# Routing without the permutation matmul: each expert's logit folded to its own and its mapped place, and the soft matmuls of the first pass moved behind both sums

## The reference

```
scores = softmax(x @ gate_w.T)                    # 64 experts
topk_w, topk_idx = top_k(scores, 8)
w_e = zeros.at[topk_idx].add(topk_w)              # the 8 largest stay, at ties the lower index
flat = w_e[:, inv_map]                            # 8 groups x 8, an index map given as input
scalar = flat.sum(-1)                             # per group
soft = softmax(where(flat == 0, -1e9, flat))      # per group
xg = x + soft @ mask_up_w                         # per group
g, u = xg @ gate_proj_w.T, xg @ up_proj_w.T       # per group, 352 inner features
y = sum over groups of scalar * ((silu(g) * u) @ down_proj_w.T)
```

## Time and profile before

| | us |
|---|---|
| median of 3 runs | 1885.43 (1883.06 to 1886.68) |
| profiled execution | 1883.3 |
| its span | 1881.6 |
| TensorE busy | 1856.3 (99%) |
| VectorE busy | 802.2 (43%) |
| ScalarE busy | 528.2 (28%) |
| GpSimd busy | 140.0 (7%) |
| mean granted TensorE clock | 0.997 |

### The profile page before, as it was taken

How to read it: one execution, slowest core, us unless ns; L and a number is a source line. 1 busy time by engine, 2 the same in 40 slices (tenths; PEclk the granted TensorE clock), 3 DMA queues, 4 the chain that set the end, 5 groups by cost and what they waited for, 6 DMA issues and landing times.

```text
span 1881.6 us, 22831 instructions
## 1 busy us (share of the span) xinstructions
PE 1856.3 (99%) x8896; PEld 1552.5 (83%) x8896; DVE 802.2 (43%) x1478; ACT 528.2 (28%) x802; POOL 140.0 (7%) x246
## 2 busy tenths in 40 slices
PE   6999999999999999999999999999999999999999
PEld 5887888888888888888888888888888888888887
DVE  6455553545354543323334455354544323322222
ACT  3333423433124432112212533123432111311111
POOL 1131110100000000000010000000000000000000
PEclk9999999999999999999999999999999999999999
DMA  6987875445564455576676454564455566567665
GB/s 198 318 279 247 276 283 199 154 156 179 191 232 151 159 172 193 193 248 210 210 254 222 164 193 163 188 231 168 156 173 179 200 239 214 210 214 261 220 235 175
DMA packets 94187, 390.68 MB, mean 208 GB/s; under 512 B 11936, under 2 KB 12320, under 8 KB 71552
## 3 DMA queue, kind: packets, MB, share of 16 engines
q1 hardware_dynamic: 54096, 286.74, 43.1%
q10 hardware_dynamic: 27600, 47.15, 9.6%
q0 software_dynamic: 12384, 55.32, 7.8%
HBM read 347.36 MB, written 41.81 MB: 207 GB/s over the span
## 4 chain that ended last, share of the span: by engine, by line
PE 94%; DVE 3%; DMA 1%; ACT 1%; issue 1%; SPq 0%; ACTq 0%; DVEq 0%
PE bank L1012 27%; PE bank L1014 27%; PE bank L1013 27%; PE bank L1244 4%; PE bank L1022 1%; PE bank L1185 1%; PE bank L1177 1%; PE bank L1184 1%; DMA b_all<-wgu 1%; PE bank L1171 1%; DVE act_t L655 0%; PE bank L1042 0%; PE bank L1229 0%; PE bank L1043 0%; PE bank L1230 0%
## 5 line engine op out<-in xcount | busy, mean ns | idle before, releaser
L1012 PE MATMUL bank<-x_hi,wt 128*128 128x512 f32 x1328 | 525.2, 395 | 0.2 <-issue 0.2
L1014 PE MATMUL bank<-x_lo,wt 128*128 128x512 f32 x1328 | 518.5, 390 | 0.0
L1013 PE MATMUL bank<-x_hi,wt 128*128 128x512 f32 x1328 | 518.2, 390 | 0.0
L655 DVE TENSOR_TENSOR act_t<-bank,sig 128x512 f32<-128x512 f32 x176 | 121.6, 691 | 557.9 <-PE bank L1244 556.3
L1014 PEld LDWEIGHTS bank<-x_lo,wt 128*128 128x128 f32 x1328 | 249.5, 188 | 53.0
L1012 PEld LDWEIGHTS bank<-x_hi,wt 128*128 128x128 f32 x1328 | 249.8, 188 | 49.9 <-issue 0.6
L1013 PEld LDWEIGHTS bank<-x_hi,wt 128*128 128x128 f32 x1328 | 249.9, 188 | 49.1
L1012 PE MATMUL bank<-dt,a_hi 128*128 128x512 f32 x704 | 279.7, 397 | 0.3 <-DVE a_lo L655 0.3
L1014 PE MATMUL bank<-dt,a_hi 128*128 128x512 f32 x704 | 275.4, 391 | 0.0
L1013 PE MATMUL bank<-dt,a_lo 128*128 128x512 f32 x704 | 274.6, 390 | 0.0
L581 ACT ACTIVATE sig<-bank 128x512 f32<-128x512 f32 x176 | 105.3, 598 | 479.4 <-PE bank L1244 479.4
(11 more groups left out here) (178 smaller groups left out, 1748.5 us busy)
## 6 DMA issues: line engine op xcount, KB each, us to landing
wt<-scr_w SPq DMA_DIRECT2D x154, 1152.0 KB, 5.2
dt<-scr_d SPq DMA_DIRECT2D x154, 512.0 KB, 5.2
s_bc<-scr_s ACTq DMA_DIRECT2D x128, 256.0 KB, 5.3
state<-wat POOLq DMA_DIRECT2D x28, 512.0 KB, 5.3
scr_w<-wt POOLq DMA_DIRECT2D x12, 1024.0 KB, 5.1
b_all<-wgu SPq DMA_DIRECT2D x22, 512.0 KB, 7.4
scr_d<-dt POOLq DMA_DIRECT2D x22, 512.0 KB, 7.1
scr_w<-tw POOLq DMA_DIRECT2D x10, 1024.0 KB, 4.7
```

Source lines behind the costliest of these rows:

```text
L655: return nc.vector.tensor_tensor(dst, a, b, op)
L1012: mm(dst, wh, xh, start=start, stop=False)
L1013: mm(dst, wl, xh, start=False, stop=False)
L1014: return mm(dst, wh, xl, start=False, stop=stop)
```

## The change

`fold_m` gets 128 columns: in the first 64, as before, the sum of both halves of the logits; in the other 64 the logit of the expert that `inv_map` puts at that place. So VectorE has own and mapped logits side by side, and the turn, its copy, the permutation matmul and the copy out of PSUM (k = 43, 44) go. The top 8 are found on the own probabilities. A mapped probability stays if it is above the eighth largest, or equal to it with an index low enough (`rank`, `cut`). The probabilities are twice as wide, and `rank` and the wider `perm_i` are loaded and prepared at the start.

In pass 0 the soft matmul of the gate moves behind the up sum. SyncE loads the gate/up tile of the next chunk ahead of the down tile of this one. The m part of chunk 2 is made in round 0 and not in round 1. The loads of x for blocks 1 and 2 move from chunks 2 and 4 to 4 and 7. The first attention slab is loaded ahead of the stores of finished blocks (`first_slab`).

```diff
-        fold_m = sb("fold_m", [P, E])
+        fold_m = sb("fold_m", [P, 2 * E])
...
+            raw_gate_up(0)
+            raw_down(0)
             sp.dma_start(mask.rearrange("p a b -> p (a b)"), c_mask).then_inc(ld_mask, 16)
-            raw(1)
+            raw_gate_up(1)
+            raw_down(1)
+            raw_gate_up(2)
             for c in range(2, CH):
-                raw(c)
-                if c == 2:
-                    sp.dma_start(xr(1), x_t[1]).then_inc(ld_x[1], 16)
-                if c == 4:
-                    sp.dma_start(xr(2), x_t[2]).then_inc(ld_x[2], 16)
+                if c + 1 < CH:
+                    raw_gate_up(c + 1)
+                raw_down(c)
+                if c in (4, 7):
+                    b = (4, 7).index(c) + 1
+                    sp.dma_start(xr(b), x_t[b]).then_inc(ld_x[b], 16)
...
             for q in range(1, PHASES):
+                if q in ATT:
+                    first_slab(ATT[q])
                 if FINAL[q - 1]:
                     store_out(q - 1)
...
+            act.dma_start(rank[:, 0, :], c_rank.partition_broadcast(P)).then_inc(ld_perm, 16)
...
                     round_a(n)
+                    if n == 0:
+                        m_top(2)
...
-                    tt(r_b, logits, bcast(mx, E), ALU.subtract).then_inc(rmax_ok, 1)
+                    tt(probs, logits, bcast(mx, 2 * E), ALU.subtract).then_inc(rmax_ok, 1)
                 elif k == 41:
+                    own, mapped = probs[:, :, 0:E], probs[:, :, E:2 * E]
+                    stt = nc.vector.scalar_tensor_tensor
                     dve.wait_ge(exp_ok, p + 1)
-                    step(nc.vector.tensor_reduce(sm, r_b, AX.X, ALU.add))
+                    step(nc.vector.tensor_reduce(sm, own, AX.X, ALU.add))
                     step(nc.vector.reciprocal(sm, sm))
-                    step(tt(r_a, r_b, bcast(sm, E), ALU.mult))
+                    step(tt(probs, probs, bcast(sm, 2 * E), ALU.mult))
...
-                    tt(r_c, r_a, r_b, ALU.subtract).then_inc(top_ok, 1)
+                    for i in range(NT):
+                        ins = stt(r_a[:, i, :], r_b[:, i, :], top[:, i, TOPK - 1:TOPK], rank[:, 0, :], ALU.is_equal, ALU.mult)
+                    step(ins)
+                    for i in range(NT):
+                        stt(r_c[:, i, :], mapped[:, i, :], top[:, i, TOPK - 1:TOPK], mapped[:, i, :], ALU.is_gt, ALU.mult)
+                    step(nc.vector.tensor_reduce(cut[:], r_a, AX.X, ALU.max))
+                    for i in range(NT):
+                        ins = stt(r_a[:, i, :], rank[:, 1, :], cut[:, i:i + 1], mapped[:, i, :], ALU.is_gt, ALU.mult)
+                    step(ins)
+                    for i in range(NT):
+                        ins = stt(r_a[:, i, :], r_a[:, i, :], top[:, i, TOPK - 1:TOPK], r_a[:, i, :], ALU.is_ge, ALU.mult)
+                    step(ins)
+                    step(tt(r_c, r_c, r_a, ALU.max))
                 elif k == 44:
-                    dve.wait_ge(flat_ok, p + 1)
-                    step(nc.vector.tensor_copy(r_c, W1[:, 0:NT * E].rearrange("p (t e) -> p t e", t=NT)))
...
                     gate(n)
+                    if n == 0:
+                        m_mask(2)
                     pieces(3 * n + 1)
                     rest_a(n)
+                    if n == 0:
+                        m_rest(2)
...
                     for i in range(NT):
-                        ins = mm(W1[:, cols(i, E)], lgT[:, cols(i)], fold_m[:], start=True, stop=True)
+                        ins = mm(W1[:, cols(i)], lgT[:, cols(i)], fold_m[:], start=True, stop=True)
                     ins.then_inc(folded, 1)
-                elif k == 43:
-                    pe.wait_ge(top_ok, p + 1)
-                    for i in range(NT):
-                        ins = nc.tensor.transpose(W1[0:E, cols(i)], r_c[:, i, :], ident[:])
-                    ins.then_inc(wT_ok, 1)
-                elif k == 44:
-                    pe.wait_ge(wT_cp, p + 1)
-                    for i in range(NT):
-                        ins = mm(W1[:, cols(i, E)], w_eT[:, cols(i)], perm[:], start=True, stop=True)
-                    ins.then_inc(flat_ok, 1)
...
-                    soft(g_bank(n), 0, p, c).then_inc(g_ok, 1)
+                    if p:
+                        soft(g_bank(n), 0, p, c).then_inc(g_ok, 1)
                     pieces(3 * n)
                     if n > 1:
                         pe.wait_ge(t1_ok, n if n > 2 else 1)
                         main(UB, P, p, c)
+                    if p == 0:
+                        soft(g_bank(n), 0, p, c).then_inc(g_ok, 1)
                     soft(u_bank(n), P, p, c).then_inc(u_ok, 1)
```

More of the change, by code:

```diff
@@ L96, in build @@
         ident = sb("ident", [P, P])
-        fold_m = sb("fold_m", [P, E])
+        fold_m = sb("fold_m", [P, 2 * E])
         reset = sb("reset", [P, NB])
[L99 to L102, removed]
+        perm_i = sb("perm_i", [P, E], I32)
+        perm_w = sb("perm_w", [P, E])
+        rank = sb("rank", [P, 2, E])
+        iota = sb("iota", [P, 1])
+        cut = sb("cut", [P, NT])
         stats = sb("stats", [P, NT, 6])
@@ L141, in build @@
         tb_flat = tb[:].rearrange("p a b -> p (a b)")
[L142 to L145, removed]
+        probs = tb_flat[:, 0:2 * NT * E].rearrange("p (t e) -> p t e", t=NT)
+        r_a, r_b, r_c = (tb_flat[:, i * NT * E:(i + 1) * NT * E].rearrange("p (t e) -> p t e", t=NT) for i in range(2, 5))
+        route = tb_flat[:, 5 * NT * E:5 * NT * E + NT * 2 * P].rearrange("p (t c) -> p t c", t=NT)
+        lgT = tb_flat[:, 5 * NT * E + NT * 2 * P:5 * NT * E + NT * 2 * P + NB]
         e_pos, e_neg, e_rest = tb[:, 0:2, :], tb[:, 2:4, :], tb[:, 4:6, :]
@@ L245, in _, with raw_gate_up @@
         def _(sp):
-            def raw(c):
+            def raw_gate_up(c):
                 j, half = c // 2, c % 2
@@ L249, in raw, with raw_down @@
                 sp.dma_start(raw_gu[:, half, :], wgu[half, j]).then_inc(raw_gu_in[half], 16)
+            def raw_down(c):
+                j, half = c // 2, c % 2
                 wait(sp, d_lo_ok, c - 1)
@@ L326, in load_t, with first_slab @@
                 pool.dma_start(raw_t, wat[s]).then_inc(raw_t_in, 16)
-            def attention(t, q):
+            def first_slab(t):
                 if t == 0:
@@ L334, in attention @@
                 load_t(t, S_V)
+            def attention(t, q):
                 rstd_of(LN_T[t])
@@ L648, in _ @@
                     pieces(3 * n + 2)
-                    if p == 0 and 0 < c < CH - 1:
+                    if p == 0 and 1 < c < CH - 1:
                         m_top(c + 1)
@@ L967, in _ @@
             gu_lo(1)
-            dve.wait_ge(ld_perm, 32)
+            dve.wait_ge(ld_perm, 48)
             dve.wait_ge(ld_id, 16)
[L970 to L976, removed]
-            nc.vector.tensor_scalar(perm[:], perm[:], iota[:, 0:1], None, ALU.is_equal).then_inc(perm_ok, 1)
+            tt(fold_m[:, 0:E], ident[:, 0:E], ident[:, E:P], ALU.add)
+            step(nc.vector.tensor_copy(perm_w[:], perm_i[:]))
+            step(nc.vector.tensor_scalar(rank[:, 1, :], perm_w[:], 0.0, float(E), ALU.is_lt, ALU.mult))
+            step(tt(perm_w[:], perm_w[:], rank[:, 1, :], ALU.add))
+            nc.vector.tensor_scalar(rank[:, 1, :], perm_w[:], -1.0, float(E), ALU.mult, ALU.add)
+            nc.vector.tensor_scalar(fold_m[:, E:2 * E], perm_w[:], iota[:, 0:1], None, ALU.is_equal).then_inc(fold_ok, 1)
             for k in range(37, 43):
@@ L1278, in _ @@
             main(UB, P, 0, 0)
-            router(0, 43)
             masked(1)
-            pe.wait_ge(perm_ok, 4)
-            router(0, 44)
             main(g_bank(1), 0, 0, 1)
@@ L1355 @@
         "c_reset": np.broadcast_to((np.arange(NB) % CK != 0).astype(np.float32), (P, NB)),
-        "c_iota": np.arange(E, dtype=np.float32)[:, None],
+        "c_iota": (row % E).astype(np.float32)[:, None],
+        "c_rank": E - np.arange(E, dtype=np.float32),
     }
```

24 lines of the change are left out of this document (10 added, 14 removed).

## The result

Median 1887.38 us (1885.84 to 1888.72) against 1885.13 for the kernel before on the same chip: ratio 1.0013 [1.0008, 1.0019]. So it is 0.13% slower, beyond its interval, where 0.5% less time was forecast: 1875.3, range 1871 to 1882. The profiled execution took 1886.81 us.

The account below looks back on a forecast made before the run. TensorE, busy 99% of the span, was taken as the bound. Terms -8.0 (passes 1 to 6), -9.1 (start) and +7.0 (rest of pass 0) made -10.1 us: 1873.2 from the 1883.3 execution, 1875.3 as median, range 1871 to 1882.

Parts of the forecast that it names:

- Part 3: Start, up to chunk 3: new pause before the scalars, but chunk 2's 6.09 us pause and slow clock go; 9.1 us gained.
- 2.7 us pause: Start: TensorE, ready at 29.5, waits for VectorE's longer router before the scalars; all behind it is 1.3 us later.
- Part 4: Rest of pass 0 from chunk 3: late soft matmul, masked waits and chunk 13's pause; 7.0 us lost.
- Chunk 11's wait: Pass 0, chunk 11: an x_lo part delays gu_lo, which ends 4.8 behind the soft matmul, TensorE there at 3.5; 1.3 us.
- Chunk 13: Pass 0: k = 41 delays chunk 14's m part; pause of 4.6 us, loss 3.3, plus 1.4 for the fallen clock.
- Part 2: VectorE's longer router: 3.6 us added (bounds 3.1 and 5.9), 16 operations 0.15 apart making 2.7; hidden in passes 1 to 6.
- Part 1: TensorE's routing work: turns and perm matmuls go, fold grows by 0.05; 1.34 us per router, 8.0 in passes 1 to 6.
- (a): Rival: the clock falls in the 2.7 us pause at the start too, costing 2.5 us: 1877.8; chance 0.20.
- (b): Rival: full DMA queues land a raw tile or store 5 us late; the start gives 4: 1880.4; chance 0.12.
- (c): Rival: small operations overlap, chunk 13's pause stays under 4 with clock up, masked never waits: 1871.3; chance 0.12.
- (d): Rival: gu_lo behind the late silu costs 0.75 us a chunk in pass 0, chunks 3 to 20: 1889.2; chance 0.05.
- (e): Rival: small operations chain at 0.31, 2.6 us more at the start and in chunk 13 each: 1883.0; chance 0.08.

Follow-up runs that it names:

- e2: The changed kernel with the rank row loaded through GpSimd's queue instead of ScalarE's: 1883.58 us, 0.9998 of the kernel before.
- e4: The changed kernel with ScalarE's three last constant loads (reset, bias, wn) issued behind the logit copy: 1882.57 us, 0.999 of the kernel before.
- e3: The kernel before with only the rank row added as an unused third small load on ScalarE's queue: 1888.64 us, 1.0027 of the kernel before.
- e1: The changed kernel, but SyncE waits for the logit copy before issuing chunk 3's raw gate/up tile: 1885.34 us, 1.001 of the kernel before.
- e5: e4 with the m tile steps ahead of k = 41 on VectorE, at the start and in chunks 13 and 14: 1875.76 us, 0.9949 of the kernel before.
- e10: The kernel before with chunk 2's m part in round 0, the new raw load order and x loads moved, no routing change: 1875.47 us, ratio 0.9949.
- e11: The kernel before with chunk 2's m part in round 0 and the old order of raw loads: 1885.75 us, ratio 1.0.
- e6: e4 with the gate's soft matmul of pass 0 back ahead of the up sum: 1874.46 us, 0.9943 of the kernel before.
- e7: e4 with GpSimd's order changed in chunk 20, store_m(20) ahead of store_w(21): 1878.02 us, 0.9961 of the kernel before.
- e8: e4 with the edits of e5 and e6, and chunk 1's up sum ahead of the scalars' turns: 1869.06 us, 0.9917 of the kernel before.
- e9: e8 with the store order of e7 as well: 1867.31 us, 0.9909 of the kernel before.

## Why the prediction was wrong

**The step that failed** is the bracket of Part 3: "The setup chain for `fold_m` and the third small load end before the logit copy, at no cost; cover about 0.1 and 6 us." It priced when the load lands, and not what it does to the issues that stand ahead of the copy on ScalarE. The logit copy came 5.3 us late, the fold 5.2, and the clock fell (0.50 in 24 to 30). In e2 and e4, without the load or with the issues moved away, the copy waits for TensorE again. The load alone makes 2.2 us of it in the kernel before (e3), and holding off the raw tile takes 1.9 off (e1); how the load, the tile and the two wider loads share the rest, and why an issue takes longer, stays open.

**Part 3's second miss.** The 2.7 us pause was put ahead of the scalars. Ahead of that, `masked(1)` needs `m_mask(0)`, which is behind k = 41 on VectorE: what is queued behind the longer instruction was named for passes 1 to 6 and not for the start. The pause was 2.57 in the kernel after and 4.34 in e4, both with a clock at 0.6 behind them; e5 takes it away. The two misses make the scalars 10.63 us late for 1.3. The rest of Part 3 was right in kind and nearly in size. Its 9.1 were net of the 1.3 that the scalars would be late, so from the scalars to the fold of pass 0 it had 10.4; e10 gains 9.9 there. e11, without the new order of the loads, gains nothing: TensorE then waits in chunk 3 for the raw tile.

**Part 4.** `masked` in ordinary chunks: a chunk takes 9.80 us for 9.61, 0.19 for the 0.15 forecast. Chunk 11's wait was 0.94 for 1.3. Yet the late soft matmul costs 4.1 us up to the fold (127.08 against e6's 123.01), where these terms make 2.2 (six chunks by 0.15, and 1.3). Measured singly they give about 2.1. The other 1.9 is the pause at 140.25, in front of the turns of x in chunk 10. On VectorE `gu_lo(11)` (137.00) stands behind the late silu (135.42), the products of chunk 10 behind it (138.14, 138.86), and the layer norm of x behind them (139.47), for which TensorE waits:

```profile
137.00 1.22 DVE L669 TENSOR_TENSOR tw<-b_all,tw 128x1024 fp32r<-128x1024 f32 x1 [2.17 <-ACT tw L410]
...
139.47 1.21 DVE L722 TENSOR_SCALAR o_all<-x_res,mv,rstd 128x512 f32<-128x512 f32 x2
```

All six kernels with the late soft matmul (after, e1, e2, e4, e5, e7) have this pause, of 1.88 to 1.90 us, and none of the other eight has one above 0.4 us there. So the forecast followed `gu_lo` to `masked` and missed what is queued behind it on VectorE. Chunk 13 was right: a pause of 5.31 for 4.6, and 4.3 us lost for 4.7, with the clock fallen as forecast. Left out was the end of pass 0. The late gate reaches, through `gu_lo(21)`, `store_w(21)` and `store_m(20)`, the first load of pass 1: a pause of 3.05, and 5.2 us in that stretch. I had looked for what `masked` needs of the tile, not for its store; e6 and e7 show this chain from two sides.

**Part 2.** VectorE in chunk 13 of the kernel after, from k = 41's first reduce to `m_mask(14)`:

```profile
178.75 0.41 DVE L760 TENSOR_REDUCE r_s<-tb 128x4 f32<-128x256 f32 x1
...
181.69 0.87 DVE L771 SCALAR_TENSOR_TENSOR tb<-tb,top,rank 128x64 f32<-128x64 f32 x4
...
...
186.11 0.42 DVE L669 TENSOR_TENSOR gt<-bank,q_all 128x256 f32<-128x256 f32 x1
```

Four in 0.87 at 0.28 each are 0.20 apart, not 0.15. The step takes 7.4 us for 3.0, 4.35 more and not 3.6, within the bounds. The 16 operations take 0.8 more than the 2.7 of the forecast, which is the whole difference. By the Trainium skill (VectorE: DVE Perf Modes, on the trn2 errata) each operation with an SBUF source pays a fixed extra latency. The spacing of 0.20 here lies between the 0.13 of the MAX8 row and the 0.28 that one of these operations lasts, so neighbours overlap in part. In passes 1 to 6 it is hidden, as forecast; those show no wait of a product.

**Part 1.** The sign was right and the size small: 1.69 to 1.78 us in each of passes 1 to 6 for 1.34, 10.4 in six for 8.0. The fold of 128 columns takes as long as that of 64, 0.81 us to the next matmul in both kernels (429.41 to 430.22, and 415.56 to 416.37 before), so the 0.05 was nothing:

```profile
429.41 1.05 PE L1079 MATMUL bank<-fold_m,tb 128*128 128x128 f32 x8
```

The other 0.3 us lie beyond the removed instructions' own spacing; what they are, no run tells.

**Rivals.** (a): the clock did fall at the start, though behind other pauses; in e5, which has the pause that (a) spoke of, it stayed up. (b): no pause for the raw tiles of chunks 3 to 5. (c) did not come: `masked` waits and chunk 13's pause is above 4. Nor did (e): the spacing is 0.20 and not 0.31. (d), the slower one, had a right cause, `gu_lo` behind the late silu, and the wrong victims: `masked` in each chunk, and not a layer norm in chunk 10 and a store at the end. Its 1889.2 lies nearest to the result, but by luck: most of the miss is at the start, of which (d) says nothing. The sum by stretch, forecast against measured, misses by 9.3 at the start, 2.6 up to the fold of pass 0 and 4.6 at its end, less 2.4 in the later passes and 0.4 in chunk 13: 13.7, the distance from -10.1 to the measured +3.5 within rounding.

## What to carry to other kernels

A DMA issue is an instruction of its engine: when a load is added, list what stands behind it on that engine, and look at the durations of the issues, not only at the landing. When one engine's step grows, follow every instruction behind it to its waiter, at the start and at the turns between passes as well, where an order that is harmless in the steady state decides; five small moves of order (e4 to e8, together in e9), one of which takes a part of the change back, turned no gain into 0.9% here. And a pause costs more than its length where the clock falls behind it.

## What was not expected of the hardware

One more small load on ScalarE's queue made the issues behind it take 1.36 to 1.87 us for 0.45 (e3: 1.90 for the last). With the load on GpSimd's queue (e2) they stayed at 0.44 and 0.45. Part of it comes back when a large load elsewhere is held off (e1: 0.74, 1.51, 1.27). The clock fell at pauses of 4.37 and 2.57 us in the kernel after, and not at those of 2.96 and 3.41 in e5; it fell near one of 1.89 in e4 and not at that of 1.88 in the kernel after. For the 3.41, and the flow behind it, e5's windows read 1.00:

```profile
250.00:255.00 5.00, 1.59 (x8) 1.04 (x7) 2.00 (x4) 1.15 (x2) 1.06 (x2) 1.00 0.99 270
255.00:258.00 3.00, 3.00 (x14) 2.47 (x15) 0.00 (x0) 0.00 (x0) 0.00 (x0) 1.00 0.76 271
```

The length of a pause alone doesn't decide it; what does is left open.
